# A layer of attention and mixture of experts on one core: the experts' weights split one expert a step, and the second half's tokens mixed five tiles in four steps

## The reference

```python
x = _layernorm(x + attention(x))            # 16 heads, ALiBi, causal
xf = x.reshape(-1, 128)                     # 8192 tokens
shared = silu(xf @ sg.T) * (xf @ su.T) @ sd.T        # hidden width 352
probs = softmax(xf @ gate_w.T)              # 8 experts
topw, topi = top_k(probs, 2); topw = topw / topw.sum(-1)
routed = sum over the two chosen experts of w * (silu(x@g_e.T) * (x@u_e.T) @ d_e.T)
x = _layernorm(x + shared + routed)
```

## Time and profile before

| | us |
|---|---|
| median of 3 runs | 1214.93 |
| lowest and highest run | 1207.92, 1221.93 |
| the profiled execution's own time | 1221.95 |
| its span | 1220.2 |
| PE busy / DVE / ACT / GpSimd (POOL), of the span | 1049.4 / 826.3 / 730.3 / 695.8 |
| mean granted clock of PE | 0.954 |

### The profile page before, as it was taken

How to read it: one execution, slowest core, us unless ns; L and a number is a source line. 1 busy time by engine, 2 the same in 40 slices (tenths; PEclk the granted TensorE clock), 3 DMA queues, 4 the chain that set the end, 5 groups by cost and what they waited for, 6 DMA issues and landing times. The chain is left out here.

```text
span 1220.2 us, 28794 instructions
## 1 busy us (share of the span) xinstructions
PE 1049.4 (86%) x9396; PEld 713.9 (59%) x9396; DVE 826.3 (68%) x2070; ACT 730.3 (60%) x1577; POOL 695.8 (57%) x1191
## 2 busy tenths in 40 slices
PE   1577989998989899888888986997999999999991
PEld 0243444444444444344344433787999999999871
DVE  2567788888888888898889832573433334666585
ACT  1116666666667665466666665445777777788542
POOL 1004444554555454377677775377888888788531
PEclk9958999999999998799999998998999999999996
DMA  5734334433453334155334222412223222445233
GB/s 94 77 46 73 59 76 85 73 66 75 77 83 69 73 74 75 44 90 100 78 93 88 59 59 68 191 35 59 79 75 79 74 79 83 116 134 142 89 111 91
DMA packets 124625, 100.42 MB, mean 82 GB/s; under 512 B 19936, under 2 KB 115430, under 8 KB 124034
## 3 DMA queue, kind: packets, MB, share of 16 engines
q1 hardware_dynamic: 114642, 76.49, 31.9%
q0 software_dynamic: 8704, 16.87, 4.2%
q10 hardware_dynamic: 1136, 5.23, 1.3%
HBM read 37.82 MB, written 35.79 MB: 60 GB/s over the span
## 5 line engine op out<-in xcount | busy, mean ns | idle before, releaser
L711 ACT ACTIVATE probs<-scores 128x512 f32<-128x512 f32 x640 | 346.7, 599 | 110.0 <-PE scores L624 108.5
L774 POOL TENSOR_SCALAR_AFFINE_SELECT probs<-probs 128x256 f32<-128x256 f32 (+1 forms) x640 | 235.6, 381 | 255.8 <-ACT probs L711 246.1
L601 PE MATMUL maxed<-kstack,qstack 52*128 52x128 bf16 (+3 forms) x1152 | 224.5, 300 | 70.3 <-DMA kstack<-parts 36.6
L624 PE MATMUL scores<-qstack,kstack 64*128 64x128 bf16 (+3 forms) x1024 | 238.9, 305 | 43.2 <-DMA qstack<-mparts 17.6
L1227 DVE TENSOR_TENSOR e_hid<-e_gate,e_up_ps 128x352 f32<-128x352 f32 (+2 forms) x192 | 107.5, 560 | 184.6 <-ACT e_gate L1506 159.7
L921 DVE TENSOR_REDUCE maxA<-maxed 128x4 f32<-128x512 f32 x256 | 165.5, 682 | 86.4 <-PE maxed L608 85.8
L640 PE MATMUL pv<-probs,vaug 128*32 128x512 f32 (+3 forms) x2048 | 200.1, 464 | 2.9 <-POOL probs L774 2.9
L921 DVE TENSOR_REDUCE maxB<-maxed 128x4 f32<-128x512 f32 x256 | 162.1, 680 | 4.5 <-PE maxed L608 4.4
L1601 POOL DMA_INDIRECT y_tokens<-e_raw,e_row_i x144 | 142.8, 991 | 37.7 <-issue 26.6
L624 PEld LDWEIGHTS scores<-qstack,kstack 64*128 64x128 bf16 x1024 | 75.9, 94 | 150.6 <-ACT probs L711 82.2
L606 PE MATMUL maxed<-causal,halves 64*128 64x256 bf16 (+1 forms) x640 | 160.0, 261 | 0.0
(11 more groups left out here) (189 smaller groups left out, 1839.6 us busy)
## 6 DMA issues: line engine op xcount, KB each, us to landing
qstack<-parts SPq DMA_DIRECT2D x192, 64.0 KB
kstack<-parts SPq DMA_DIRECT2D x192, 64.0 KB
x_sorted<-zeros SPq DMA_DIRECT2D x16, 580.5 KB, 10.2
e_xs<-x_sorted SPq DMA_DIRECT2D x144, 64.5 KB
e_raw<-y_tokens SPq DMA_DIRECT2D x64, 128.0 KB
xin<-in_x SPq DMA_DIRECT2D x16, 256.0 KB, 3.2
e_group_in<-x1T_all SPq DMA_DIRECT2D x16, 256.0 KB, 3.0
out<-e_raw SPq DMA_DIRECT2D x64, 64.0 KB
```

What stands on the lines that cost most here:

```text
L601: pe.matmul(bank[:, at:at + (k1 - k0) * P], q[rows, slot, i * P:(i + 1) * P], ks[rows, slot, k0 * P:k1 * P], start=first, stop=False, skip ...
L624: last = pe.matmul(scores[st.at(0, SEQ_UNITS, n) % SB][:, col:col + width], ks[rows, slot, kt * P:(kt + 1) * P], q[rows, slot, kt * P:T], ...
L711: act.activation(probs[g % 2][:, u * T:(u + 1) * T], scores[st.at(0, SEQ_UNITS, UNITS * g + u) % SB][:], ACT.Exp).then_inc(S["exp_done"], 1)
L774: pool.affine_select(out=view, in_=view, compare_op=ALU.is_ge, fill=0.0, base=0, pattern=pattern, channel_multiplier=-1).then_inc(S["maske ...
```

## The change

Each of steps 10 to 17 splits one whole expert: ACT keeps the high parts of gate and up, GpSimd the rest of gate, DVE the rest of up, placed between its addition into x1 (line 1241) and the routing arithmetic. The mixing of the second chunk goes from three steps for four turns from step 176 to four steps for five turns from step 173. NORM_LAG becomes 9, the rings 12 tiles, the ring of evicted results (YTURN) 26, and TOKENS_A_STEP 0.75. The load of the last sequence's input moves from SP's step -5 to its step -1, and GpSimd's addition to it from step 0 to step 1.

```diff
-NORM_LAG = 7
+NORM_LAG = 9
-MTURN = 8
+MTURN = 12
-MIX = ((PARTED + CSLOT + 24, 3, 2), (PARTED + NSLOT + 8, 3, 4))
-SPLIT_AT = 8
+MIX = ((PARTED + CSLOT + 24, 3, 2), (PARTED + NSLOT + 5, 4, 5))
+SPLIT_AT = 10
-YTURN = 27
+YTURN = 26
-WRITES_A_STEP, NORM_TAKES, TOKENS_A_STEP = 1.4, 0.7, 0.8
+WRITES_A_STEP, NORM_TAKES, TOKENS_A_STEP = 1.4, 0.7, 0.75
...
-            return divmod(step - SPLIT_AT, 2) if 0 <= step - SPLIT_AT < 2 * NE else None
+            return step - SPLIT_AT if 0 <= step - SPLIT_AT < NE else None
...
-                    dve.tensor_tensor(w_in[:, e, w, 1, :], shared_in[:, w, :], w_in[:, e, w, 0, :].bitcast(F32),
-                                      ALU.subtract).then_inc(S["shared_rest"], 1)
+                    whole = shared_in[:, w, :] if e == NE else raw[:, e, w, :]
+                    dve.tensor_tensor(w_in[:, e, w, 1, :], whole, w_in[:, e, w, 0, :].bitcast(F32),
+                                      ALU.subtract).then_inc(S["shared_rest" if e == NE else "up_rest"], 1)
+                    if split_at(step) is not None:
+                        keep_rest(split_at(step), 1)
...
-                    if step == STEPS[0]:
+                    if step == -1:
                         sp.dma_start(last_in[:], ...)
...
-                            pe.wait_ge(S["weight_rest"], 2 * NE)
+                            pe.wait_ge(S["gate_rest"], NE)
+                            pe.wait_ge(S["up_rest"], NE)
...
-                    if split_at(step):
+                    e = split_at(step)
+                    if e is not None:
                         act.wait_ge(S["experts_loaded"], EXPERTS_IN)
-                        keep_high(*split_at(step))
+                        for w in range(2):
+                            keep_high(e, w)
...
-                def keep_rest(e, w):
-                    pool.wait_ge(S["weight_kept"], 2 * (e + 1) + w + 1)
-                    pool.tensor_tensor(w_in[:, e, w, 1, :], raw[:, e, w, :], w_in[:, e, w, 0, :].bitcast(F32),
-                                       ALU.subtract).then_inc(S["weight_rest"], 1)
+                def keep_rest(e):
+                    pool.wait_ge(S["weight_kept"], 2 * (e + 1) + 1)
+                    pool.tensor_tensor(w_in[:, e, 0, 1, :], raw[:, e, 0, :], w_in[:, e, 0, 0, :].bitcast(F32),
+                                       ALU.subtract).then_inc(S["gate_rest"], 1)
-                    if step == LAST["yn"]:
+                    if step == LAST["o"] - 1:
-                            four = slice(quad % 2 * QT, quad % 2 * QT + QT)
+                            four = slice(quad % (MTURN // QT) * QT, (quad % (MTURN // QT) + 1) * QT)
-                            if quad >= 2:
-                                pool.wait_ge(S["result_ready"], QT * (quad - 1))
+                            if quad >= MTURN // QT:
+                                pool.wait_ge(S["result_ready"], QT * (quad - MTURN // QT + 1))
```

More of the change, by code:

```diff
@@ L1098, in experts @@
         group_ps = [h_ps, y_ps]
-        names = """const_loaded experts_loaded const_set weight_kept weight_rest routed chosen prefix_ps prefix_kept placed places
+        names = """const_loaded experts_loaded const_set weight_kept gate_rest up_rest routed chosen prefix_ps prefix_kept placed places
             exponents exponents_done weighted experts_set ids_set x_scattered row_ready x_ready xT_kept xT_rest gate_ready up_ready
@@ L1607, in _ @@
                     last_chain(step)
-                    if split_at(step):
-                        keep_rest(*split_at(step))
+                    if split_at(step) is not None:
+                        keep_rest(split_at(step))
                     group, part = part_at(step + TURNED, (0,))
```

## The result

The changed kernel took 1221.25 us in the median of 20 runs (1215.24 to 1228.11), the kernel before 1214.69 us (20 runs, 1207.92 to 1224.69). The ratio is 1.0056, with a 95% interval of 1.0029 to 1.0082: 3.5 to 10 us slower, 6.6 us in the medians, where +2.0 us was forecast. The profiled execution took 1224.43 us, with a span of 1222.7 us (before: 1220.2).

What follows compares the result with a forecast made beforehand. PE, busy 86% of the span, was taken to bound the kernel outside its stalls. Weights and input load -6.2, tokens +12.2, second mixing -4.0 gave +2.0 us on the median 1214.93: 1216.9 us, range 1205 to 1226.

Steps and rivals of the forecast that it cites:

- B: Tokens, steps 27 to 94: the later last token makes PE stand still at tile 72, then run slowly; +12.2 us.
- C: Second mixing: it starts at about 1150.3 instead of 1155.24 us and the last aggregation ends earlier; -4.0 us.
- The seven writes: Before token 64, GpSimd has seven more writes at 1.47 us each, without slack to make them up; 10.3 us.
- A, the rests: Weights, steps 8 to 24: GpSimd's rests shared with DVE start step 24 2.9 us earlier and save 2.3 us of slow clock.
- 4.96 for the standstill: Before step 24: PE's wait of 4.96 us for GpSimd's last weight rest goes.
- 0.3 for step 21: At step 21: a wait of some 0.3 us for GpSimd goes with its load.
- 2.3 for the clock: Behind PE's wait before step 24: the stretch at lower clock goes too, 2.3 us won.
- the second rival: Steps 11 to 15: DVE's up rests collide with GpSimd's, 1.45 us each instead of 0.47; +4.9, sum +6.9, 1221.8 us; chance 0.10.
- A, the load of the last input: Start of the experts: the last sequence's input load moves behind both first groups' loads; 1.0 us won (0 to 1.7).
- the third rival: Second mixing wins nothing: DVE's standstill or the late group load reaches PE; sum +6.0, 1220.9 us; chance 0.07.
- DVE's standstill: Step 173, second mixing: DVE waits about 2 us for its load, and PE, two steps ahead, hardly feels it.
- Rival 1: Steps 27 to 94: the tokens cost nothing, GpSimd makes up seven writes or the load lands in time; 1204.7 us; chance 0.13.

Runs made afterwards that it cites:

- the kernel with the tokens back: The changed kernel with tokens at 0.8 a step and the results' ring at 27 tiles again: 1206.54 us, ratio 0.9919 to the kernel before.
- the second run with 0.78: The changed kernel with tokens at 0.78 a step instead of 0.75, on a chip with routed steps of 2.08 us: 1220.43 us, ratio 1.0002 to the kernel before.

## Why the prediction was right, and where its terms were off

**Right: the sign of every term and the stretch in which it lies, and the size of B.** The time lies in the range, but a range of 15 us is wide beside a change of 6.6. The sum was 3.3 us too low in the pieces (5.26 against 2.0), most of it in C; another 1.3 us separate the pieces from the medians.

**B, +12.2, measured +12.11 and +12.09.** PE's row at tile 72, SP's wait of 14.4 us (about 15 was said), the clock behind and the lost lead of GpSimd were all as described. That the size agrees to 0.1 us is luck, for the parts are off by more. The seven writes did cost 10.4 us (I had 10.3), but the wait for the second result added 0.8 and the hidden landing before the copy took 1.4 away, neither of which I had worked out: 9.8 us. PE's transpose of tile 72 came 9.1 us late, where I had 9.9; and behind it another 3.0 us were lost by hid 140 (2.7 of them within three steps, at the low clock), where I had 2.3.

**A, the rests, -5.2, measured -4.74.** The piece splits at hid 20. Behind it, 7.8 us were won (23.99 to 16.23), where 4.96 for the standstill, 0.3 for step 21 and 2.3 for the clock make 7.6. Before it, 3.0 us were lost (29.44 to 32.46), where I had 2.35. The under-sized term is "I take 0.47 each", with "I add none" for the collisions: four of the eight rests met GpSimd's operations and took 2.6 us more than their 0.52 together. That is the mechanism of the second rival at about a quarter of its price: of the five rests that I had counted two were stretched, by 1.2 us where the rival has 4.9; the other two are the one of step 10, with slack behind it, and the longest, of 1.46 us, which lies behind hid 16 and for whose hid PE doesn't wait. Hid 20 came 0.65 us later than forecast. I was also wrong on the place: PE's long wait is in step 15, for the hid of step 13, not in step 18. The slow clock behind that wait is not what cost the 0.65 us. In five of the nine traces with these rests the clock stayed at 1.00 behind the same wait (2.15 or 2.16 us); PE then waited for the hids of steps 15 and 16 instead, as here in the kernel with the tokens back,

```profile
812.02 0.93 PE L1406 MATMUL e_gate_ps<-e_group_x,e_w_in 128*96 128x512 f32 x3 [0.96 <-DVE e_hid L1228]
```

and step 24 started 40.0 us behind hid 8, against 39.9 in the four where the clock fell. VectorE sets the pace there, and what PE loses by its clock it would have waited. The rests moved to steps 16 to 23 gave back 2.0 us by hid 20, and 1.3 by step 24, where PE then waited for the last of them. The Trainium skill ("SBUF — State Buffer", section "Who interferes with whom") speaks of an exclusive lock between a VectorE instruction with two SBUF inputs and a GpSimd instruction that reads SBUF; the rows agree: each long rest ends 0.4 us behind GpSimd's operation, none of the others is stretched, and a part of that rival belonged in the forecast.

**A, the load of the last input, -1.0, measured -0.59 in the one pair of traces and near -0.2 over all.** ACT waits for the first group 3.81, 3.68, 3.59 and 1.71 us with the old order, and 3.40 to 3.96 with one of 1.74 in the ten traces with the new one; the medians of these waits differ by 0.2 us, which is no more than their scatter. The load behind which the other stood was not what made it slow. I had compared its landing with the median of loads at other places.

**C, -4.0, measured -1.88 in the changed kernel, -3.3 to -3.7 with other timings.** The start of the mixing was better than I said (5.9 us earlier, not 4.9). What failed is "PE is two steps ahead and hardly feels it": the hid of step 174 stands in DVE's queue behind the mix of tile 33, and PE waited 2.41 us for it, then worked at a lower clock. The single collision that I priced at 0.8 us lies there, where it costs PE's time too. So the third rival (C = 0) held half: DVE's standstill did reach PE, but only 2 of 4 us were lost. That the standstill was the size in question was shown by taking it away, which gave the whole piece 1.5 us less than the 73.7. The waits for 1/std shrank as forecast in the four quads with a hid between: 0.26 us in three, none in one.

**Rival 1** (the tokens cost nothing) fell where PE's routed steps take 2.08 us, but it is what happened on the chips where they take more: there PE never waited for tile 72, and the changed kernel was 0.7% faster. The prediction had treated the pace of PE as given.

## What to carry to other kernels

A planner's rate is a due time: before you lower it, count the writes ahead of the one that somebody waits for, and multiply by the engine's measured time for one; seven writes of an engine without slack cost 12 us, more than both other edits won together. Then look for the waits inside that order: the same two kinds of writes in another order gained 1.4 us or lost 1.3 by whether one stood between a scatter and the wait for its landing. When work is moved to another engine, place it by that engine's gapless stretches and by what the neighbour on the shared memory does at that moment: the same eight operations in later steps cost 1.2 to 1.3 us less by step 24, and would have to end earlier to be worth the 2.0 us that they had won by hid 20. Where a step's first load is behind others in a queue, put the loads that the chain waits for first.

## What the runs showed of the hardware that was not expected

**The same program, 7% apart by the chip.** The kernel before has medians of 1214.7, 1218.9 and 1220.9 us, and 1307.2 and 1302.6 us. The first part and the shared steps take the same time on all; the routed steps don't. The windows 836 to 980 of the changed kernel in its first trace and on the slower chip (us, then busy us and count of PE, PEld, DVE, ACT, POOL, PEclk), and who waited there on the slower one:

```profile
836.00:980.00 144.00, 134.83 (x1035) 132.98 (x1033) 53.46 (x204) 100.51 (x263) 121.00 (x150) 0.99 0.27 74
```

```profile
836.00:980.00 144.00, 111.14 (x695) 101.27 (x693) 38.17 (x141) 63.77 (x175) 107.28 (x133) 0.91 0.21 60
...
DVE e_hid L1228 <- remote: 37.2, 10, 5.3
...
PEld e_y_ps L1472 <- issue: 19.0, 19, 2.3
```

PE did two thirds of the work in the same time, and PE, ACT and DVE alike wait for nothing that the profile can name ("issue", "remote"), in some stretches and not in others. What it is stays open; no run here was made for it. It decides what an edit is worth: the tokens' 12 us don't exist there.

**The part before the experts.** In 14 traces, whose code up to there differs at most in the place of one load, the experts' first matmul lies anywhere from 748.5 to 765.3 us. That is as wide as the spread of the single runs of the kernel before (1207.92 to 1224.69 us). Behind it, pieces in which no load's landing decides repeat to 0.1 us: hid 28 to 140 took 234.84, 234.85, 234.84 and 234.84 us in four kernels.

**A collision is settled by who begins first.** A mixing operation of VectorE that began 0.10 us ahead of GpSimd's group rest (at 1152.46 in the second run with 0.78) took its usual 0.35 us, and GpSimd's operation took 1.37 instead of 1.26; in the changed kernel one that began with it took 1.41.

**The clock behind one and the same wait.** PE waits 2.15 or 2.16 us before step 15 in nine traces. In four of them the 3.45 us behind it had a mean granted clock of 0.65 to 0.71, in the other five 1.00.
